# Two-layer graph network: the attention weights in one VectorE instruction from PSUM, and divisions and normalizations on ScalarE

## The reference, cut to what matters

```
# layer 0: x (8, 2048, 256), adj (8, 2048, 2048) of 0 and 1
idx   = the first 25 neighbours of each row (top_k of -j where adj[i, j] != 0)
agg   = max over x[idx]; where the degree is 25 or less, max(agg, 0)
x     = layernorm(x + relu(concat([x, agg]) @ W0 + b0))
# layer 1: 4 heads of 64
h     = x @ W1[head]
e_src, e_dst = h . a_src, h . a_dst          # one type of edge occurs: adj is 0 or 1
weight = leaky_relu(e_src[i] + e_dst[j], 0.01), -1e9 where adj[i, j] == 0
dst   = softmax(weight) @ h + bias
out   = relu(dst) + h
out   = (out - mean) / sqrt(var + 1e-6) * gamma + beta      # over the 64 of a head
x     = layernorm(x + out)
```

## Time and profile before

| | |
|---|---|
| three timed runs | 5440.72, 5489.24, 5507.57 us (median 5489.24) |
| the profiled execution | span 5448.3 us; its time with what lies around the span is not given apart |
| busy, share of the span | VectorE 4138.1 us (76%), GpSimd 3717.1 (68%), TensorE 3438.2 (63%), ScalarE 3111.4 (57%) |
| granted TensorE clock, mean | 0.778 |
| DMA | 692.71 MB, mean 127 GB/s |

### The profile page before, as it was taken

The page is one execution under the profiler, slowest core; times in us unless marked ns, Lnnn a source line. Parts: engine busy times, 40 slices in busy tenths (PEclk is TensorE's granted clock), DMA queues, the critical chain, the costliest instruction groups (busy, mean ns, idle before and its releaser), DMA issues.

```text
span 5448.3 us, 58256 instructions
## 1 busy us (share of the span) xinstructions
PE 3438.2 (63%) x11778; PEld 1438.1 (26%) x11778; DVE 4138.1 (76%) x11484; ACT 3111.4 (57%) x5570; POOL 3717.1 (68%) x3204
## 2 busy tenths in 40 slices
PE   1232467666666767666676666666666666666786
PEld 1121222222222222222222222222222222222222
DVE  4555578878787888878787878888878788787777
ACT  3333456666556666656655655656656666555565
POOL 4666777777777777777777777777777777677400
PEclk9555578777778777878777787787888778778798
DMA  3434344444444444444444444444444444444210
GB/s 113 130 119 136 119 138 128 146 132 146 125 129 133 135 144 135 132 143 129 134 133 133 145 125 127 139 130 146 136 144 131 128 139 131 137 131 133 85 39 27
DMA packets 282021, 692.71 MB, mean 127 GB/s; under 512 B 62849, under 2 KB 130178, under 8 KB 265346
## 3 DMA queue, kind: packets, MB, share of 16 engines
q0 software_dynamic: 153600, 419.64, 26.1%
q1 hardware_dynamic: 128130, 270.41, 15.6%
HBM read 639.21 MB, written 50.59 MB: 127 GB/s over the span
## 4 chain that ended last, share of the span: by engine, by line
POOL 36%; issue 25%; DVE 22%; PE 8%; DMA 4%; ACT 3%; another core or an unknown queue 1%; POOLq 0%; DVEq 0%; SPq 0%; ACTq 0%
POOL rows L498 36%; PE acc L1231 5%; DVE uv L819 5%; DVE rmax L836 4%; DMA rows<-in_x_dram,idx 4%; DVE top L715 2%; DVE key_b L717 1%; PE pB L1199 1%; DVE agg L845 1%; DVE sth L892 1%; ACT uv L565 1%; DVE key_a L717 1%; DVE mvh L898 1%; ACT stage L525 0%
## 5 line engine op out<-in xcount | busy, mean ns | idle before, releaser
L498 POOL DMA_INDIRECT rows<-in_x_dram,idx x3200 | 3716.9, 1162 | 1404.5 <-issue 997.0
L1231 PE MATMUL acc<-uv,hs 128*65 128x512 f32 x4096 | 2301.4, 712 | 707.2 <-DVE uv L819 448.3
L565 ACT ACTIVATE uv<-rb,qj 128x512 f32 (+1 forms) x2048 | 1330.4, 712 | 169.6 <-PE acc L1231 137.6
L819 DVE SCALAR_TENSOR_TENSOR uv<-uv,maskT 128x1024 f32<-128x1024 f32 x1024 | 1239.9, 1221 | 183.6 <-ACT uv L565 148.4
L1231 PEld LDWEIGHTS acc<-uv,hs 128*65 128x65 f32 x4096 | 602.6, 160 | 1992.7 <-issue 1403.4
L836 DVE TENSOR_TENSOR rmax<-rmax,rows 128x1280 f32<-128x1280 f32 x384 | 572.5, 1491 | 600.4 <-DMA rows<-in_x_dram,idx 553.5
L628 ACT ACTIVATE xaT<-pA 128x512 f32<-128x512 f32 x128 | 76.4, 597 | 791.3 <-PE pA L1186 610.6
L542 ACT ACTIVATE stage<-pT 128x1024 bf16<-128x1024 f16 x256 | 260.6, 1018 | 288.8 <-remote 148.0
L1186 PE MATMUL pA<-id,xt 128*128 128x128 f32 x256 | 81.5, 419 | 469.4 <-DVE agg L846 334.2
L640 ACT ACTIVATE x1T<-pA 128x256 f32<-128x256 f32 x128 | 49.2, 384 | 570.8 <-PE pA L1209 394.5
L1199 PE MATMUL pB<-w_sb,xaT 128*128 128x256 f32 x1024 | 348.0, 499 | 18.4 <-ACT xaT L628 8.6
(11 more groups left out here) (113 smaller groups left out, 3755.5 us busy)
## 6 DMA issues: line engine op xcount, KB each, us to landing
adj_sb<-in_adj_dram SPq DMA_DIRECT2D x128, 1024.0 KB
rows<-in_x_dram,idx POOLq DMA_INDIRECT x3200
xh_dram<-xh SPq DMA_DIRECT2D x128, 256.0 KB
rb<-r_dram SPq DMA_DIRECT2D x32, 1024.0 KB
xr<-xh_dram SPq DMA_DIRECT2D x64, 512.0 KB
xt<-in_x_dram SPq DMA_DIRECT2D x128, 128.0 KB
out_dram<-xr SPq DMA_DIRECT2D x32, 512.0 KB
r_dram<-er SPq DMA_DIRECT2D x128, 2.0 KB
```

The costliest lines, as they stand in the source:

```text
L498: nc.gpsimd.indirect_dma_start(rows[:, c, r * C:(r + 1) * C], None, x_rows, bass.IndirectOffsetOnAxis(ap=idx[p][:, k:k + 1], axis=0)).then ...
L565: last = nc.scalar.activation(uv[k][:, i, :], rb[:, bass.ds(qa % 2, 1), h, :].rearrange("p a i -> p (a i)"), ACT.Copy, scale=q_j(h))
L819: nc.vector.scalar_tensor_tensor(uv[k][:], uv[k][:], 1.0, m, ALU.max, ALU.mult).then_inc(s_u, 1)
L1231: last = nc.tensor.matmul(acc[h][0:HW, :], hs[:, (1 - quad.par) * JT + jt, h, :], uv[k][:, i, :], start=(jt == 0), stop=(jt == JT - 1))
```

## The change

A unit is now one block of j and the two heads of a pair; a quad's first two steps (u = 0, 1) do heads 0 and 1 (pair 0), the last two heads 2 and 3 (pair 1), over all 16 blocks. TensorE puts r of two heads into two PSUM banks `rq`, broadcast over partitions by a product with a 4 x 128 selector (`broadcast`), once a pair. `er` keeps r in SBUF; `r_dram`, its stores and the load of `rb` are gone. VectorE makes mask * max(r, 1/q) from `rq` in one instruction per head (`masked`, two halves of 512 a unit), and writes `uv`; the factor q goes into h (the exponent of `dj` is 1 in place of 0.01). ScalarE's `scaled` is gone. All 16 halves of a step stand inside the search.

The sums go back once a pair (twice a quad): `numerators` on ScalarE (two instructions), `back` on TensorE as 8 products with `backmat` (identity of 65, with the bias in its last row, so that sum*bias is added before the division), `divide` on VectorE (two reciprocals), `quotients` on ScalarE (8 instructions of 64, relu and scale) into `raw`. `heads_norm` (16 instructions of 64) and `rows_norm` (4 of 256) on ScalarE take the place of lines 909, 918 and 964. The reduction of 5 rows is three maxima of 512, 256 and 256.

```diff
-            def scaled(quad, u, n, ahead=0):
...
-                    last = nc.scalar.activation(uv[k][:, i, :], rb[:, bass.ds(qa % 2, 1), h, :].rearrange("p a i -> p (a i)"),
-                                                ACT.Copy, scale=q_j(h))
+            def numerators(quad, pair):
+                for v in quad.reach(lambda q: UNITS * (q - lag) + last_unit):
                     act.wait_ge(s_pe, v)
...
+                for i in range(PAIR):
+                    last = nc.scalar.activation(sT[:, i, :], acc[i][0:HW, :], ACT.Identity, bias=tiny[0:HW, :])
+                last.then_inc(s_sT, 1)
+            def quotients(quad, pair):
+                for v in quad.reach(lambda q: 2 * (q - lag) + pair + 1):
+                    act.wait_ge(s_rden, v)
...
+                        last = nc.scalar.activation(raw[:, i, c:c + HO], acc[i // 2][:, at:at + HO], ACT.Relu,
+                                                    scale=rden[:, pair, i // 2, i % 2 * PAIR + h:i % 2 * PAIR + h + 1])
+                last.then_inc(s_accfree, 1)
+            def heads_norm(quad):
...
+                        last = nc.scalar.activation(dst[:, i, c:c + HO], dst[:, i, c:c + HO], ACT.Identity,
+                                                    scale=rsh[:, k:k + 1], bias=nbh[:, k:k + 1])
+                last.then_inc(s_normh, 1)
+            def rows_norm(quad):
...
+                    last = nc.scalar.activation(xr[:, i, :], dst[:, i, :], ACT.Identity, scale=rsf[:, i:i + 1], bias=nbf[:, i:i + 1])
```

```diff
-                for v in quad.reach(lambda q: UNITS * (q - BQ) + US * u + n + 1):
-                    dve.wait_ge(s_v, v)
-                m = maskT[:, bass.ds((quad.q - BQ) % RING * JT + jt, 1), :].to_broadcast([P, 2, IB])
-                nc.vector.scalar_tensor_tensor(uv[k][:], uv[k][:], 1.0, m, ALU.max, ALU.mult).then_inc(s_u, 1)
+                if i == 0:
+                    for v in quad.reach(lambda q: UNITS * (q - BQ) + US * u + n - UVB + 1):
+                        dve.wait_ge(s_pe, v)
+                    if n == 0:
+                        dve.wait_ge(s_proj, projected(quad, u))
+                        if u % 2 == 0:
+                            for v in quad.reach(lambda q: 2 * (q - BQ) + pair + 1):
+                                dve.wait_ge(s_rq, v)
...
+                stt = nc.vector.scalar_tensor_tensor(uv[k][:, i, :], rq[i][:], inv, m, ALU.max, ALU.mult)
...
-                ch.then(nc.vector.tensor_reduce(agg[:], rmax[:].rearrange("p (r f) -> p f r", f=C), axis=AX.X, op=ALU.max))
+                ch.then(nc.vector.tensor_tensor(rmax[:, 0:2 * C], rmax[:, 0:2 * C], rmax[:, 2 * C:4 * C], ALU.max))
+                ch.then(nc.vector.tensor_tensor(rmax[:, C:2 * C], rmax[:, C:2 * C], rmax[:, 4 * C:5 * C], ALU.max))
+                ch.then(nc.vector.tensor_tensor(agg[:], rmax[:, 0:C], rmax[:, C:2 * C], ALU.max))
...
-            UNIT_AT = (2, 4, 6, 14, 22, 31)
+            UNIT_AT = (3, 4, 5, 6, 9, 13, 14, 18, 21, 22, 23, 25, 28, 30, 31, 33)
```

The finish on VectorE is now: step 1, place 16 `raw` + h, then statistics at 20 and 24; step 2, place 16 reciprocal, 18 a small product (`nbh`), 29 a wait for `heads_norm` and gamma; step 3, beta at 16, x at 18, statistics at 20 and 24, behind the step reciprocal and `nbf`. TensorE's step begins:

```diff
             def step(quad, u):
+                if quad.on(u, QT * BQ):
+                    pe.wait_ge(s_proj, projected(quad, u))
+                    if u % 2 == 0:
+                        broadcast(quad, u // 2)
                 if u == 0 and quad.on(u, FIN):
-                    back(quad)
+                    back(quad, 1)
+                if u == 2 and quad.on(u, QT * BQ):
+                    back(quad, 0)
                 if quad.on(u, 1):
                     product0(quad, u)
...
+                if quad.on(u, QT * BQ) and u % 2 == 0:
+                    for v in quad.reach(lambda q: 2 * (q - BQ) + u // 2):
+                        pe.wait_ge(s_accfree, v)
                 attend(quad, u, 0, 4)
```

`broadcast` waits until VectorE has done all units of the pair before (they read the same `rq`), and its operands have 4 rows and 512 columns:

```diff
+            def broadcast(quad, pair):
+                for v in quad.reach(lambda q: UNITS * (q - BQ) + pair * UNITS // 2):
+                    pe.wait_ge(s_u, v)
...
+                for i in range(PAIR):
+                    last = nc.tensor.matmul(rq[i][:], headsel[:, PAIR * pair + i, :],
+                                            er[0:HEADS, bass.ds((1 - quad.par) * N + block, IB)], start=True, stop=True)
+                last.then_inc(s_rq, 1)
```

More of the change, by code:

```diff
@@ L52 @@
 US = UNITS // QT
+PAIR = 2
+HJ = JT // 2
 UVB = 4
-AHEAD = 3
 BIG = 3.0e38
@@ new lines, in heads_norm @@
+            def heads_norm(quad):
+                for v in quad.reach(lambda q: q - BQ):
+                    act.wait_ge(s_nbh, v)
+                for i in range(QT):
+                    for h in range(HEADS):
+                        k, c = i * HEADS + h, h * HO
+                        last = nc.scalar.activation(dst[:, i, c:c + HO], dst[:, i, c:c + HO], ACT.Identity,
+                                                    scale=rsh[:, k:k + 1], bias=nbh[:, k:k + 1])
+                last.then_inc(s_normh, 1)
@@ L574, in step @@
+            def rows_norm(quad):
+                for v in quad.reach(lambda q: q - BQ - 1):
+                    act.wait_ge(s_nbf, v)
+                for i in range(QT):
+                    last = nc.scalar.activation(xr[:, i, :], dst[:, i, :], ACT.Identity, scale=rsf[:, i:i + 1], bias=nbf[:, i:i + 1])
+                last.then_inc(s_out, 1)
             def step(quad, u):
-                next_attends = quad.on(u, QT * BQ - 1)
-                if quad.on(u, QT * BQ) or next_attends:
-                    act.wait_ge(s_proj, projected(quad, u))
+                if u == 0 and quad.on(u, FIN + QT):
+                    rows_norm(quad)
@@ L579, in step @@
                 if u == 0 and quad.on(u, FIN):
[L581 to L588, removed]
+                    numerators(quad, 1)
@@ L589, in step @@
+                if u == 2 and quad.on(u, QT * BQ):
+                    numerators(quad, 0)
                 if quad.on(u, -2):
                     mask(quad, u, 2)
+                if u == 0 and quad.on(u, FIN):
+                    quotients(quad, 1)
+                if u == 2 and quad.on(u, QT * BQ):
+                    quotients(quad, 0)
                 if quad.on(u, 1):
@@ L986, in between @@
                     if fin and u == 0 and place == DIVIDE_AT:
-                        divide(quad)
+                        divide(quad, 1)
+                    if att and u == 2 and place == DIVIDE_AT:
+                        divide(quad, 0)
                     if behind and place in NORM_AT:
```

238 lines of the change are left out of this document (104 added, 134 removed).

## The result

The changed kernel took 6814.27 us (median of 4 runs, 6808.14 to 6817.05) beside 5472.44 us of the kernel before (5440.72 to 5507.57): 1.244 times as long, 95% interval 1.237 to 1.252. Predicted were 5426 us and at most 5600. The profiled execution took 6808.14 us and spans 6806.3.

A forecast was written before the change was run, and what follows sets the result against it. A loop through GpSimd's gathers and VectorE's search was taken to bound, 40.0 us a tile. Steps of 39.2 over 110 tiles gave -88, early stretch +5, tail +20: 5385 us for the profiled execution, 5426 against the median; range 5220 to 5600.

The forecast's parts named there:

- So the new halves cost GpSimd nothing: VectorE's mask halves read one input from PSUM, so gathers beside them were to stay at 0.95 us.
- the 34.1 us of gathers: GpSimd's 25 gathers of a tile after the change; bounds 33.2, and 38.2 if the halves block all the same.
- the 1.8 to 2.4 us that I had put down to late landings: Excess of the 40.0 us step over the loop's computed conditions, ascribed to late-landing rows and VectorE coming late.
- round trips that reach `idx`: Rival: slow broadcast, back and product0 at pair heads delay idx; mean step 41.2, total 5661 us; chance 0.15.
- `residual` at 10.6, place 12 at 13.7: Heads of steps 0 and 2: times in us, place 12 coming 0.8 late, caught up by chunk 3.
- the second rival: Pair round trips reach idx: residual at 16, place 12 at 19, steps 41.5 and 44, total 5661 us; chance 0.15.
- from about 2 us of delay on: Delay of the pair's round trip at which the rival of round trips reaching idx was to decide.
- Heads on ScalarE, 3.5 us, wait of 1.8: Sixteen heads_norm instructions at 0.22 us each; wait at place 29, on the loop, 1 to 2.7, taken as 1.8.
- Steps 1 and 3: A quad's second and fourth steps, forecast 39.2 and 39.5 us from gathers, landings and VectorE's work behind chunk 1.
- A half unit at 0.683: VectorE's 512-column half: 683 ns, 0.60 us behind another instruction; 16 a step 9.6 us against 9.1.
- the tail: Behind the last gather TensorE paces; a second change a quad costs 28 us, less 8: +20, from 290 to 310.
- if the waits for rows are gone and steps stay above 40, VectorE bounds: Sign that the assumed 12.9 us of VectorE slack ahead of place 12 was wrong.

The follow-up runs named there:

- e6_both: Changed kernel with heads_norm ahead of project, product0 ahead of back and divide at place 11: ratio to before 1.211 on chip 4, 1.220 on chip 15.
- c2_before: The kernel before, nothing edited, profiled on chip 3: 5324.2 us.
- e1b_sbuf: Changed kernel with ScalarE copying r from PSUM to SBUF once a pair and the halves reading the copy, on chip 10: 6578.2 us beside 5485.1 of before.
- c1_after: The changed kernel, nothing edited, on chip 3: 5360.8 us, ratio 1.0036 to the kernel before.
- e3_late: Changed kernel with product0 ahead of back on TensorE and divide at place 11 in place of 6, on chip 12: 5268.1 us beside 5361.8 of before.
- e6e_both: Changed kernel with heads_norm ahead of project, product0 ahead of back and divide at place 11, on chip 3: 5112.2 us, ratio 0.957 to before.

## Why the prediction was wrong, point by point

**The step that failed** is "So the new halves cost GpSimd nothing", with the 34.1 us of gathers taken as a gain alone. In length it was right (33.6 us on chip 3, 31.4 to 33.2 by steps in the result). The sum had no term for what closer gathers do to the other engines. Where the result was measured, `back` came up to 22 us late and `product0` of two steps in four only behind the last gather, and the turn was 52.2 us for the 39.2 forecast. GpSimd's own breaks take that away: on chip 15 `e6_both` has 1.220 without them and 1.015 with four a tile.

The trace of before had signs of it. In the early stretch links of the search came late behind VectorE's own instructions, and a tile took 37.75 us, where it is 34.4 on chip 3; I took both as they were. In the full stretch the stall is only about 0.5 us of the 1.8 to 2.4 that I had put down to late landings and to VectorE coming late: `c2_before` has 39.5 for 40.0, so the rest is there without it. And before the change `divide` started 2.3 to 5.7 us behind `back`'s first record, on a chip that stalls, beside gathers of 36.9 us for 25.

That it was the missing interruptions of `uv` which let the stall grow to 12 us fits these numbers, but isn't shown: `e1b_sbuf`, which put some back, mended a fifth of it. None of my rivals had this. The nearest, round trips that reach `idx`, had the place right and gave 41.5 and 44 us for steps that took 57.2 and 61.8.

**Where a chip doesn't stall** the prediction can be held to its terms. There the change is +0.4%, 22 us, for the -1.2% forecast; that it came out so near is luck in part, since steps 0 and 2 were 3.3 and 3.5 us longer than forecast and steps 1 and 3 were 1.0 and 2.9 shorter. Steps of a quad, from first gather to first gather, means over 24 quads:

| | step 0 | 1 | 2 | 3 | mean |
|---|---|---|---|---|---|
| before, chip 3 | 38.3 | 41.8 | 38.6 | 39.0 | 39.4 |
| predicted | 37.3 | 39.2 | 39.9 | 39.5 | 39.0 |
| `c1_after`, chip 3 | 40.6 | 38.2 | 43.4 | 36.6 | 39.7 |
| `e3_late`, chip 12 | 36.7 | 38.1 | 43.7 | 36.6 | 38.8 |
| `e6e_both`, chip 3 | 36.9 | 38.1 | 37.6 | 36.7 | 37.3 |
| `after`, the result | 57.2 | 47.0 | 61.8 | 43.0 | 52.2 |

- *`residual` at 10.6, place 12 at 13.7.* Measured 14.8 and 14.0 in steps 0 and 2 (us behind the start of L862, which is L846 of before), and place 12 at 17.5 and 16.8: the second rival, which had 16 and 19 and steps of 41.5 and 44. `broadcast` came 1 us later than I had it, `back` took the upper of my ends (3.5), and `product0` its 4 us behind it. The rival's condition, "from about 2 us of delay on", was met. With `product0` ahead of `back` (`e3_late`) `residual` stands at 10.6 to 10.8 and place 12 at 13.6, and the first step is 36.7.
- *Heads on ScalarE, 3.5 us, wait of 1.8.* Sixteen take 5.4: L579 reads SBUF and comes every 0.34 us, where L663's kind, my row, comes every 0.22. The wait ahead of gamma was 3.0 us. Setting `heads_norm` ahead of `project` took the wait away (L931 in `c1_after`, then in `e6e_both`), and from `e3_late` to `e6e_both` the third step fell from 43.7 to 37.6.

```profile
L931 DVE TENSOR_TENSOR dst<-dst,gamma_b 128x1024 f32<-128x1024 f32 x32 | 39.2, 1224 | 85.1 <-ACT dst L579 85.1
```

```profile
L931 DVE TENSOR_TENSOR dst<-dst,gamma_b 128x1024 f32<-128x1024 f32 x32 | 38.9, 1215 | 5.5 <-ACT dst L579 5.5
```

- *Steps 1 and 3* came 1.0 and 2.9 us better than forecast: the gathers and the first one of the next tile decide there, 34.1 and 4.05, 33.8 and 2.8 us. Which of my terms was too long was not tried.
- *A half unit at 0.683.* It is 0.740, 0.06 more; for sixteen that is 0.9 us a step.
- *Reading of the rows:* 25 gathers of before take 36.9 us and not 37.3, 0.4 less.
- *Held:* ScalarE under 2200 us (2186), the wait for `broadcast` at place 3 (4.6 us each time in `c1_after`, 5 forecast), the gather's mean (1.050 in the full stretch of chip 3, 1.06 forecast), the three maxima off the loop (L859 to L861 behind `idx`), and the tail: 344 us on chip 3 beside 326, +18 for +20.

Of "what would show it", "if the waits for rows are gone and steps stay above 40, VectorE bounds" named the picture but not its cause: VectorE's waits for rows fell from 726.1 to 274.8 us in the result, and it is idle 41% of the full stretch.

## What to carry to other kernels

Closer gathers aren't a gain alone: before a change brings GpSimd's gathers nearer together, look in the trace for instructions that come late by whole gathers behind their own engine's last one. Profile the unchanged kernel on a second chip before a surprise of this size is explained by the program; here the count of gathers in one early stretch told the kinds apart, and so did the number of semaphore updates in the trace. And with several round trips at the head of a step, put first on TensorE what the rest of the step waits for: that order, with `divide` moved behind it and one queue position on ScalarE, is the difference between 1.004 and 0.957.

## What the runs showed of the hardware

- Chips 4, 7, 10 and 15, and that of the result (its number isn't known), hold up work of TensorE and VectorE beside gathers by GpSimd 1.25 us apart, as their recorded runs show it; chips 3 and 12 don't. The same program takes 6814 us on one and 5361 on another, or 6566 to 6621 and 5112 (`e6_both`). The kernel before differs only by 2%. Whether that difference is the chips' own or comes with the recording on them is open.
- The records of TensorE don't show it: products have records close behind one another, and only the semaphore, or the instruction that waits for it, tells that they were complete up to 22 us later.
- On chip 3 a chunk's rows have landed 1.7 to 1.8 us behind the end of its last gather (`c1_after`, the middle half of 640 chunks); where the stall is, the records of landings are incomplete. In the stall of tile 52 the core loads no instructions between 2524.4 and 2578.0 us, so it doesn't wait for those. What is held up, and where, stays open; that breaks of GpSimd end it is shown; whether their length, their number or the mean rate counts is not.
- Four breaks cost 4 us a tile, and with them this chip's kind takes 1.015 of before. So on such a chip no version tried beats the kernel before; on the others `e6` does, by 4.3%.
